# A fused transformer block on one core: another order of first-stage transfers, an earlier store of the first shift row, and LayerNorm roots spread between the sequences

## The reference, cut to what matters

```python
def ref(x):                                   # x: (8, 256, 128) float32
    x = x + diff_attention(layernorm(x))      # Wq, Wk, Wv (128x256), Wo (256x128), lambdas, rms_scale
    x = x + ffn(layernorm(x))                 # W1 (128x512), W2 (512x128)
    x = x + linear_attention(layernorm(x))    # bWq, bWk, bWv, bWo (128x128)
    x = x + ffn(layernorm(x))
    return x

# diff_attention: 16 heads, two maps each (32 maps), causal softmax;
#   attn = softmax(A1) - lam * softmax(A2), lam = exp(sum lq1*lk1) - exp(sum lq2*lk2) + 0.8
#   O = attn @ V, RMS-normed, times rms_scale * 0.2, then @ Wo
# ffn weights: w = softmax(top-k logits) over 32 primitives (k = 32, so all of them)
#   W1 = sum_k w1[k] * fc1_A[k] @ fc1_B[k]    # fc1_A 32x128x64, fc1_B 32x64x512
#   W2 = sum_k w2[k] * fc2_A[k] @ fc2_B[k]    # fc2_A 32x512x64, fc2_B 32x64x128
```

## Time and profile before

| | us |
|---|---|
| median of three runs | 445.51 |
| time of the profiled execution | 446.8 |
| its span on the core | 445.1 |
| PE busy | 377.5 (85%) |
| DVE busy | 288.7 (65%) |
| ACT busy | 259.4 (58%) |
| POOL busy | 203.6 (46%) |
| mean share of the 16 DMA engines by the main queue | 37.2% |
| attention's first matmul starts | 80.96 |
| attention's slot 6 starts | 104.07 |

### The profile page before, as it was taken

The page is one execution under the profiler, slowest core; times in us unless marked ns, Lnnn a source line. Parts: engine busy times, 40 slices in busy tenths (PEclk is TensorE's granted clock), DMA queues, the critical chain, the costliest instruction groups (busy, mean ns, idle before and its releaser), DMA issues.

```text
span 445.1 us, 10136 instructions
## 1 busy us (share of the span) xinstructions
PE 377.5 (85%) x3380; PEld 243.8 (55%) x3380; DVE 288.7 (65%) x952; ACT 259.4 (58%) x634; POOL 203.6 (46%) x324
## 2 busy tenths in 40 slices
PE   0699688795999988888888799897888999999996
PEld 0566487672555545545454455443685566655674
DVE  6586363484889797988889697111132989999200
ACT  3333134133788787787968687877367434343832
POOL 5232224002558575675747475834002687783000
PEclk9999799895999999999999999959899999999999
DMA  8789969984554445152535400000000000000011
GB/s 211 251 275 327 260 145 211 169 157 81 76 74 74 74 75 75 41 91 39 84 45 76 73 4 3 4 1 0 0 2 2 0 0 2 0 0 1 2 48 47
DMA packets 47347, 34.51 MB, mean 78 GB/s; under 512 B 20032, under 2 KB 41664, under 8 KB 47296
## 3 DMA queue, kind: packets, MB, share of 16 engines
q1 hardware_dynamic: 47296, 33.86, 37.2%
HBM read 25.20 MB, written 8.39 MB: 75 GB/s over the span
## 4 chain that ended last, share of the span: by engine, by line
PE 41%; DVE 18%; ACT 11%; issue 11%; DMA 7%; POOL 6%; SPq 5%; DVEq 0%; POOLq 0%
PE ps L1268 5%; PE ps L1088 5%; ACT arena L820 4%; PE ps L1010 4%; DVE arena L1402 3%; DMA stacks<-arena 3%; PE ps L644 3%; DMA qk_parts<-qk_parts_sb 3%; PE ps L1259 2%; PE ps L1018 2%; DVE arena L1415 2%; PE ps L1164 2%; SPq L407 2%; PE ps L1005 2%; PE ps L1134 2%
## 5 line engine op out<-in xcount | busy, mean ns | idle before, releaser
L772 POOL TENSOR_SCALAR_AFFINE_SELECT arena<-arena 128x256 f32<-128x256 f32 (+1 forms) x192 | 90.5, 485 | 88.3 <-ACT arena L820 84.7
L820 ACT ACTIVATE arena<-ps 128x512 f32<-128x512 f32 x192 | 109.3, 604 | 28.7 <-PE ps L1044 27.3
L953 DVE TENSOR_REDUCE arena<-ps 128x4 f32<-128x1024 f32 x64 | 78.2, 1221 | 14.2 <-PE ps L1018 12.9
L946 DVE CUSTOM_DVE_ANT_0 ps<-ps,future 128x128 f32<-128x128 f32 x256 | 66.4, 320 | 22.2 <-PE ps L1005 21.9
L1044 PE MATMUL ps<-stacks 50*128 50x256 bf16 x256 | 50.9, 281 | 1.4 <-ACT arena L820 1.3
L1343 POOL TENSOR_TENSOR arena<-arena 128x1024 f32<-128x1024 f32 x16 | 34.2, 2137 | 34.3 <-DVE arena L1428 33.8
L1010 PE MATMUL ps<-stacks 48*128 48x256 bf16 x256 | 41.7, 277 | 3.4 <-ACT arena L820 2.0
L472 POOL TENSOR_TENSOR qk_parts_sb<-qk_rest,qk_parts_sb 128x512 bf16<-128x512 f32 x16 | 19.1, 1209 | 49.8 <-DVE qk_parts_sb L557 49.8
L1088 PE MATMUL ps<-arena 128*17 128x256 f32 x512 | 41.8, 400 | 0.0
L1005 PE MATMUL ps<-stacks 48*128 48x128 bf16 x256 | 25.3, 220 | 16.2 <-DMA stacks<-arena 7.2
L1471 PE MATMUL ps<-arena,upto 128*128 128x384 f32 x96 | 36.0, 487 | 0.0
(11 more groups left out here) (129 smaller groups left out, 765.0 us busy)
## 6 DMA issues: line engine op xcount, KB each, us to landing
stacks<-qk_parts SPq DMA_DIRECT2D x96, 128.0 KB, 4.5
qk_parts<-qk_parts_sb SPq DMA_DIRECT2D x16, 384.0 KB, 4.5
...
qk_parts<-qk_parts_sb SPq DMA_DIRECT2D x8, 128.0 KB, 5.1
stacks<-arena SPq DMA_DIRECT2D x64, 4.0 KB
...
```

The lines of the kernel that those rows point to most:

```text
L772: nc.gpsimd.affine_select(out=diag, in_=diag, compare_op=ALU.is_ge, fill=0.0, base=0, pattern=[[0, 2 if s < 2 else UMAPS], [1, P]], channe ...
L820: nc.scalar.activation(probs[:, r, s, :], ps[:, bank, :], ACT.Exp, scale=SCALE).then_inc(exp_done, 1)
L946: last = nc.vector.tensor_tensor_reduce(out=block, in0=block, in1=future[:], scale=1.0, scalar=LOWEST, op0=ALU.add, op1=ALU.max, accum_out ...
L953: nc.vector.tensor_reduce(out=rowmax[:, gs, 1, UMAPS * uu:UMAPS * (uu + 1)], in_=ps[:, S_BANK + 1:S_BANK + 3, :].rearrange("p b (m k) -> p ...
```

## The change

- **Order of DMAs.** fc1_B's quarter 2 is issued at once instead of behind sequence 0; quarter 3, fc2_B and the four quarters of fc2_A each move one sequence forward, and so do the stacks of groups 0 and 1 (now behind sequence 5). The thirteen small DMAs leave the front and a semaphore each takes the place of the shared one: `lam_in` stands behind fc1_B's quarter 3 in sequence 0, `wo_raw` and `rms_col` behind fc2_A's quarter 0 in sequence 2, `wb_raw` behind stack 1 in sequence 5.
- **Shift row.** The wait for all parts leaves the end of the first stage. `attend_sync` waits only for sequence 1's parts, issues stacks 2 and 3, stores the first shift row, and waits for all parts after that.
- **Roots.** ACT makes the roots of tiles 0 to 3 only before `columns(0)`, and the other three steps inside sequences 0, 1 and 2. DVE makes `rows(1)` before `first_moments(1)`, and the moments of tiles 8 to 15 behind the splits of sequences 0 and 1.

```diff
--- before.py
+++ after.py
@@ -212,7 +212,8 @@
         x_in = [sem(f"x_in{i}") for i in range(4)]
         w_in = sem("w_in")
         tick_pool, tick_dve = sem("tick_pool"), sem("tick_dve")
-        small_in, logits_in = sem("small_in"), sem("logits_in")
+        lam_loaded, wb_in, logits_in = sem("lam_loaded"), sem("wb_in"), sem("logits_in")
+        wo_in = sem("wo_in")
         rms_in = sem("rms_in")
         fc1_a_in, fc2_b_in = sem("fc1_a_in"), sem("fc2_b_in")
         fc1_b_in = [sem(f"fc1_b_in{i}") for i in range(4)]
@@ -409,16 +410,7 @@
 
             load_fc1_b(0)
             load_fc1_b(1)
-            for i, w in enumerate((bWq, bWk, bWv, bWo)):
-                sp.dma_start(wb_raw[:, i, :], w).then_inc(small_in, 16)
-            sp.dma_start(wo_raw[:, :, :], Wo.rearrange("(c p) n -> p c n", p=P)).then_inc(small_in, 16)
-            for i, w in enumerate((lq1, lk1, lq2, lk2)):
-                sp.dma_start(lam_in[:, i, :],
-                             w.rearrange("h d -> (h d)").partition_broadcast(P)).then_inc(small_in, 16)
-            for i in range(P // DV):
-                sp.dma_start(rms_col[DV * i:DV * (i + 1), :],
-                             rms_scale.rearrange("(p a) -> p a", a=1)).then_inc(rms_in, 16)
-
+            load_fc1_b(2)
             for b in range(SEQS):
 
                 sp.wait_ge(low_done, 2 * b + 2)
@@ -428,22 +420,31 @@
                 sp.dma_start(parts_dram[b, :, K0_AGAIN].rearrange("h p t -> p h t"),
                              part_of(b % 2, 1, 0)).then_inc(parts_out[b % 2], 16)
 
-                if b < 2:
-                    load_fc1_b(2 + b)
-                if b == 2:
+                if b == 0:
+                    load_fc1_b(3)
+                    for i, w in enumerate((lq1, lk1, lq2, lk2)):
+                        sp.dma_start(lam_in[:, i, :],
+                                     w.rearrange("h d -> (h d)").partition_broadcast(P)).then_inc(lam_loaded, 16)
+                if b == 1:
                     sp.dma_start(b2, fc2_B.rearrange("k r f -> (k r) f").rearrange("(c p) f -> p c f", p=P))\
                       .then_inc(fc2_b_in, 16)
-                if b == 6:
+                if b == 5:
 
                     sp.wait_ge(parts_out[0], 48)
                     sp.wait_ge(stacks_filled, 4)
                     load_stack(sp, 0, 0)
-                if 3 <= b < 7:
-                    load_fc2_a(b - 3)
-                if b == 6:
+                if 2 <= b < 6:
+                    load_fc2_a(b - 2)
+                if b == 2:
+                    sp.dma_start(wo_raw[:, :, :], Wo.rearrange("(c p) n -> p c n", p=P)).then_inc(wo_in, 16)
+                    for i in range(P // DV):
+                        sp.dma_start(rms_col[DV * i:DV * (i + 1), :],
+                                     rms_scale.rearrange("(p a) -> p a", a=1)).then_inc(rms_in, 16)
+
+                if b == 5:
                     load_stack(sp, 1, 1)
-            for u in range(2):
-                sp.wait_ge(parts_out[u], 48 * SEQS // 2)
+                    for i, w in enumerate((bWq, bWk, bWv, bWo)):
+                        sp.dma_start(wb_raw[:, i, :], w).then_inc(wb_in, 16)
 
         def project_gpsimd(pool):
             nc.gpsimd.memset(eps[:], LN_EPS).then_inc(eps_done, 1)
@@ -476,18 +477,19 @@
 
             act.wait_ge(eps_done, 1)
             load_log_exp(act)
-            for i in range(4):
-                if i == 1:
-                    act.wait_ge(w_in, 16 * 3)
-                    for side in range(2):
-                        nc.scalar.copy(wqk[:, side].rearrange("k c (d m) -> k c d m", d=DH),
-                                       wqkv[:, side].rearrange("k (c m d) -> k c d m", c=2, d=DH))\
-                            .then_inc(wqk_done, 1)
+            def first_roots(i):
                 c = slice(4 * i, 4 * i + 4)
                 act.wait_ge(moments_done, 4 * i + 4)
                 nc.scalar.activation(log_var[:, c], moments[:, c, 1], ACT.Ln, bias=eps[:, 0:1]).then_inc(log_done, 1)
                 act.wait_ge(log_done, i + 1)
                 nc.scalar.activation(rstd[:, c], log_var[:, c], ACT.Exp, scale=-0.5).then_inc(rstd_done, 1)
+
+            first_roots(0)
+            act.wait_ge(w_in, 16 * 3)
+            for side in range(2):
+                nc.scalar.copy(wqk[:, side].rearrange("k c (d m) -> k c d m", d=DH),
+                               wqkv[:, side].rearrange("k (c m d) -> k c d m", c=2, d=DH))\
+                    .then_inc(wqk_done, 1)
             def columns(b):
                 act.wait_ge(xT_done, b + 1)
                 nc.scalar.copy(xnT1[:, b % 2, :], ps[:, X_BANK, 0:SEQ]).then_inc(xnT_done, 1)
@@ -496,6 +498,8 @@
             for b in range(SEQS):
                 if b + 1 < SEQS:
                     columns(b + 1)
+                if b < 3:
+                    first_roots(b + 1)
                 if b >= 2:
                     act.wait_ge(parts_out[b % 2], 48 * (b // 2))
                 for side in range(2):
@@ -559,10 +563,8 @@
 
             first_moments(0)
             rows(0)
+            rows(1)
             first_moments(1)
-            rows(1)
-            first_moments(2)
-            first_moments(3)
             dve.wait_ge(logits_in, 16 * 2)
             for i in range(2):
                 nc.vector.tensor_reduce(out=lg_negmax[:, i:i + 1], in_=logits[:, i, :], axis=AX, op=ALU.max,
@@ -581,7 +583,7 @@
                         .then_inc(s_mix, 1)
 
             def lambdas():
-                dve.wait_ge(small_in, 16 * 9)
+                dve.wait_ge(lam_loaded, 16 * 4)
                 for i in range(2):
                     nc.vector.tensor_tensor(lam_prod[:, i, :], lam_in[:, 2 * i, :], lam_in[:, 2 * i + 1, :],
                                             op=ALU.mult).then_inc(lam_mul, 1)
@@ -597,11 +599,14 @@
                                                in1=lam_exp[:, 1, :], op0=ALU.add, op1=ALU.subtract)\
                     .then_inc(s_lam, 1)
                 dve.wait_ge(rms_in, 16 * P // DV)
+                dve.wait_ge(wo_in, 16)
                 nc.vector.tensor_scalar(wo[:], wo_raw[:], rms_col[:, 0:1], 1.0 - LAMBDA_INIT,
                                         op0=ALU.mult, op1=ALU.mult).then_inc(wo_done, 1)
 
             for b in range(SEQS):
                 split(b)
+                if b < 2:
+                    first_moments(b + 2)
                 if b + 2 < SEQS:
                     rows(b + 2)
                 if b == 0:
@@ -652,7 +657,7 @@
                                             start=True, stop=True)
                 last.then_inc(proj_done, 1)
                 factors_tensor(pe, b)
-            pe.wait_ge(small_in, 16 * 9)
+            pe.wait_ge(wb_in, 16 * 4)
             for i in range(4):
                 last = nc.tensor.transpose(ps[:, X_BANK, i * P:(i + 1) * P], wb_raw[:, i, :], ident[:])
             last.then_inc(wbT_ps, 1)
@@ -721,6 +726,7 @@
             return (SLOTS // UPG) * it + (j - L_SHIFT - 1) // UPG + 1
 
         def attend_sync(sp):
+            sp.wait_ge(parts_out[1], 48)
             load_stack(sp, 2, 2)
 
             def store_shift(g, slot):
@@ -733,8 +739,10 @@
                                      shift[HMAPS * h:HMAPS * (h + 1), slot % 2, part, :])\
                           .then_inc(shift_in[slot][h], 16)
 
+            load_stack(sp, 3, 3)
             store_shift(0, 0)
-            load_stack(sp, 3, 3)
+            for u in range(2):
+                sp.wait_ge(parts_out[u], 48 * SEQS // 2)
             for it in range(GROUPS // 4 - 1):
                 for k in range(4):
                     g = 4 * it + k
```

## The result

The changed kernel took 449.36 us (median of 4 executions, 448.79 to 450.84), the kernel before 444.06 us (4, 441.81 to 448.01: the three given ahead and one more): ratio 1.0131, 95% interval 1.009 to 1.0173. It is slower, by 1.3%; the forecast was no change. The ratios leave out single executions more than 1.5% above their kernel's fastest (five of ten in e7, four in e2b, three in e6), so a ratio can differ from that of the medians. The profiled execution of after took 448.79 us, its span was 447.1 us at a mean granted clock of 0.953.

A forecast was written before the change was run, and what follows sets the result against it. PE sets the end, with three stalls due to the DMA queue. Later attention (+5.9), no row stall (-4.47) and faster slots 6 to 8 (-1.6) gave -0.2 us: 445.3 us, own range 441.5 to 449, whole range 440 to 450.5.

The forecast's parts named there:

- the three stalls: PE's DMA waits in the first 105 us: 4.01 us for fc2_A, 4.84 for stack 0, 4.47 for the first shift row.
- the queue's sum: DMA queue up to the attention: `wb_raw` lands at 85.5 us, the attention starts at 86.9, 5.9 us later than before.
- the forward sum: The same queue added up forward, with 7.3 us for parts and a quarter: `wb_raw` lands at 84.5 us.
- The lambdas: New DVE wait near 27 us for `lam_in`, 3.0 us of queue, until 32.2; PE then stands still 4 to 5 us.
- `rms_col`: Second new DVE wait, for `wo_raw` and `rms_col` behind fc2_A's first quarter: 1.5 us of queue, landed at about 49.4.
- a second hole: Slower rival: parts of sequence 4 after 56 us or 5 after 64 run the queue dry; 449.6 us, chance 0.13.
- The start "hidden behind what follows": Moved roots at the kernel's start: worth 1 us of PE's time or up to 2 us lost, both ends hidden.
- The shift row: First row, slot 6: no stall, slot 6 at 105.5 instead of 104.07, +1.4 us; rival that it is late, 0.05.
- The row's old stall: PE's wait in slot 6 for the first shift row, taken as 4.47 us that the change removes.
- Without the stall: 1.6 us less: Slots 6 to 8 took 9.17 us at the low clock; without the stall 1.6 us less, ends 0 and 2.1.
- the faster rival: The quicker queue: `wb_raw` in before PE arrives at 75 to 77, attention at about 77.5, 436 us; chance 0.14.
- The sum: Whole kernel: +5.9 - 4.47 - 1.6 = -0.2 us on the profiled 446.8; on 445.5 this gives 445.3 us.

The follow-up runs named there:

- e7: The changed kernel with `wo_raw` and `rms_col` moved back to the front, behind fc1_B's second quarter; 447.62 us, ratio 1.002 to the kernel before.
- e2b: The kernel before with the wait for all parts moved behind the first shift row, the row still ahead of stack 3; 443.34 us, ratio 0.9973.
- e6: The changed kernel with only `lam_in` moved back to the front, behind fc1_B's second quarter; 446.69 us, ratio 1.0048 to the kernel before.
- e4: The changed kernel with roots, moments and shift row as before, so only the order of DMAs changed; 447.63 us, ratio 1.0052.
- a2: The changed kernel run again unaltered, with ten executions; 446.61 us, ratio 1.0051 to the kernel before.
- e3: The kernel before with only the change's roots and moments between the sequences; 444.19 us, ratio 0.9964.
- e1: The changed kernel with only `wb_raw` moved, to sequence 2 in front of `wo_raw`; 439.90 us, ratio 0.9896 to the kernel before.
- e8: The changed kernel with `wb_raw`, `lam_in`, `wo_raw` and `rms_col` back behind fc1_B's second quarter; 438.12 us, ratio 0.9782 to the kernel before.
- e2: The kernel before with only the change's shift row part: stacks 2 and 3, the row, then the wait for all parts; 445.12 us, ratio 1.0026.
- b2: The kernel before run again, unaltered but for two empty lines; 445.46 us over ten executions, ratio 1.002.
- e5: The changed kernel with `wb_raw` moved to sequence 2 and the first shift row stored before stack 3; 437.73 us, ratio 0.9807 to the kernel before.
- e9: As e8, and the first shift row stored before stack 3 is issued; 434.25 us, ratio 0.9731 to the kernel before.

## Why the prediction was right and wrong

- **What bounds it, the three stalls, the queue's sum**: right. The stall before the transposes of `wb_raw` ended at 84.19 and 84.36 (forecast 85.5; the forward sum 84.5 was nearer), and in e6, e7 and e4 at 84.85, 83.81 and 86.23. That it hardly moves with the waits of DVE fits a queue whose work is fixed. The attention started at 86.07 (86.9).
- **The lambdas, `rms_col`**: right in kind and place. In after fc1_B's fourth quarter landed at 29.45 (20.95 + 8.5; 29.2 in the sum) and the last lambda 1.2 us behind it, in a2 2.1, where the sum had 3.0. DVE went on at 30.70 and 31.54 instead of 32.2, and PE's stall was 2.0 and 1.8 instead of 4 to 5 us. That the eight issues of `rms_col` leave a hole of some 3 us at 46 to 50 was not foreseen: I had counted 1.5 us of queue, and looked for a second hole only at 56 and 64. With the hole at 36 to 38 us the queue lost about 4 us, where the sum had 1.6 (share 0.47, 0.06 and 0.50 in three stretches of 2 us). Other terms were too large by as much, the lambdas and the start among them; that 84.19 lies near 85.5 is in part luck.
- **The start "hidden behind what follows"**: wrong by 1 to 2 us, in the change's favour. e3 has slot 0 1.7 us sooner than before, and with the roots moved `wb_raw` comes 2 us sooner (a2 against e4). The first parts go out sooner (e3 0.85 us, above), and what follows in the queue moves with them.
- **The shift row**: right for the change, no stall and slot 6 at 105.5 (105.55). But the reason is the late start of the attention. Behind stack 3 the row is late again in e1, e8 and e2. And the 105.5 is right by luck: the attention started 0.8 us before the forecast and slots 0 to 5 took 0.8 us more (19.48 for 18.64; a2 19.98, b2 19.92).
- **The row's old stall**: the sum took the 4.47 us of one profile. The second profile of before had 2.19. Over two profiles of each kernel the change moves slot 6 by +2.3 us (105.9 against 103.6), where I had +1.4.
- **The term that failed: "Without the stall: 1.6 us less" in slots 6 to 8.** From slot 6 to slot 9 after took 9.02 us (114.57 - 105.55), before 9.17: 0.15 us less. The low clock there was put down to the stall, and it comes without one. In after the clock was at 1.00 in the stretch from 106 us, then at 0.63, 0.50, 0.50 and 0.67 in the four from 108 us on; PE was busy 1.46 and 1.00 of 2 us in the stretches from 106 and 108, waiting for DVE and ACT in slots 6 and 7 (the row at 109.00). In before, behind the stall, it was low from the start of slot 6:

```profile
108.00:110.00 2.00, 1.99 (x18) 1.13 (x18) 1.74 (x10) 1.08 (x2) 0.86 (x3) 0.50 0.00 0
```

Over all profiles, slots 6 to 8 took 8.99 to 9.51 us in the six with a stall for the row (before, b2, e1, e2, e3, e8; mean 9.26) and 7.63 to 9.02 in the eight without (after, a2, e4, e5, e9, e7, e6, e2b; mean 8.55). So the term is worth about 0.7 us in the mean, not 1.6, and 0.15 in the pair that was compared; from slot 6 to slot 13 the means are 19.29 and 18.79, 0.5 apart. Only e2b, where the clock stayed at 1.00 throughout although PE was busy as little (1.44 and 0.94 of 2 us), had the full gain: 7.63, and 17.53 up to slot 13. The sum had named 0 as this term's lower end.
- **The same reading was too cautious for slots 0 to 5.** "It costs slots 0 to 5 the same low clock as before" was right for the change, but the faster rival kept 18.64 us there too. PE is busy throughout those slots, and where its long wait ahead of them goes, they take 17.0 us (e1, e5, e8, e9): there the clock did come back.
- **The sum.** Without that term -0.2 becomes +1.4; the two profiles that were compared have slot 13 at +1.6 (124.76 against 123.12). With slot 6 at +2.3 the start of slot 13 lies at +2.1 over two profiles each (124.67 against 122.55). That is 0.5%, what a2 and e4 measured over ten executions each (medians +2.2 and +2.0 us).
- **The other 3 us of the first comparison** (449.36 to 446.61) are not explained. All four lay at 448.8 us or above, the profiled one at a clock of 0.953 against 0.969 in a2's profile, and from the start of slot 13 it took 322.3 us against 317.9 for a2 (before: 322.0, b2: 318.0). So the tail differs between executions of one kernel by as much as those 3 us, for both kernels. Why four of four fell on that side stays open: another chip (the record names none for the first comparison), or the clock's course after a later start.
- **The rivals.** The quicker queue did not occur. The second hole did, at another place, and without moving `wb_raw`. The chance for slower, 0.17, rested on holes and the row only. That the 1.6 us might not come was no rival of its own, though it alone puts the sum at +1.4 us, and with slot 6 as two profiles of each have it at +2.3.
